# One tanh for the four LSTM gates, the output bias in two later halves, filler matmuls, and 128-row mask and bias operands in a decoder layer

## The reference

```
x = x + LSTM_attention(layernorm(x))      # LSTM of width 20 over the 56 tokens; heads give mu and sigma;
                                          # causal Gaussian weights, normalised, times layernorm(x)
x = x + cross_attention(layernorm(x), ctx_1024)   # 16 heads of 64 over 1500 context rows, plus bias bO
x = x + ffn(layernorm(x))                 # a router picks 1 of 4 experts: gelu(x W1[e] + b1[e]) Wo + bo, then layernorm
```

```
i, f, g, o = split(xg_t + h @ W_hh.T)
c = sigmoid(f) * c + sigmoid(i) * tanh(g)
h = sigmoid(o) * tanh(c)
```

## Time and profile before

| | us |
|---|---|
| median of 3 runs | 1596.07 (1593.94 to 1597.94) |
| the profiled execution's own time | 1587.43 |
| span of the profile | 1585.7 |
| PE busy | 1517.7 (96%) |
| DVE busy | 1131.3 (71%) |
| ACT busy | 903.5 (57%) |
| POOL busy | 792.8 (50%) |
| granted TensorE clock, mean | 0.985 |

### The profile page before, as it was taken

How to read it: one execution, slowest core, us unless ns; L and a number is a source line. 1 busy time by engine, 2 the same in 40 slices (tenths; PEclk the granted TensorE clock), 3 DMA queues, 4 the chain that set the end, 5 groups by cost and what they waited for, 6 DMA issues and landing times.

```text
span 1585.7 us, 25257 instructions
## 1 busy us (share of the span) xinstructions
PE 1517.7 (96%) x7555; PEld 1084.1 (68%) x7555; DVE 1131.3 (71%) x1872; ACT 903.5 (57%) x1283; POOL 792.8 (50%) x406
## 2 busy tenths in 40 slices
PE   6886899999999999999999999999999999999997
PEld 3345667777777777777777777777777777776674
DVE  4338786868686868686877778686868686868555
ACT  4335675666666666666666666666666566555311
POOL 2003365555555555656565655555555555545511
PEclk9997999999999999999999999999999999999899
DMA  4100011000000000000000000000000000100000
GB/s 157 32 0 20 1 39 40 40 39 39 32 38 28 39 28 38 30 39 39 39 39 39 39 39 39 39 39 39 39 39 39 39 39 39 40 14 7 1 1 24
DMA packets 15059, 54.92 MB, mean 35 GB/s; under 512 B 919, under 2 KB 6122, under 8 KB 15022
## 3 DMA queue, kind: packets, MB, share of 16 engines
q1 hardware_dynamic: 15022, 54.46, 9.0%
HBM read 53.54 MB, written 0.92 MB: 34 GB/s over the span
## 4 chain that ended last, share of the span: by engine, by line
PE 83%; DVE 8%; ACT 5%; issue 3%; DMA 0%; DVEq 0%; POOL 0%; POOLq 0%; ACTq 0%
PE ps L725 34%; PE ps L691 27%; PE ps L597 4%; PE ps L592 3%; PE ps L583 3%; PE ps L784 3%; DVE arena L1282 3%; PE ps L576 2%; ACT arena L982 2%; PE ps L705 2%; PE ps L512 1%; PE ps L713 1%; ACT arena L881 1%; ACT arena L884 1%; DVE arena L1268 1%
## 5 line engine op out<-in xcount | busy, mean ns | idle before, releaser
L1268 DVE TENSOR_TENSOR arena<-arena,ps 125x896 f32<-125x896 f32 x336 | 364.4, 1084 | 96.3 <-PE ps L691 96.0
L449 POOL TENSOR_TENSOR arena<-arena,ring 125x896 f32<-125x896 f32 x192 | 417.6, 2175 | 17.5 <-POOL arena L449 0.5
L691 PE MATMUL ps<-q_hi,ctxT_hi 128*125 128x448 f32 x768 | 400.0, 521 | 4.7 <-ACT arena L976 3.2
L449 POOL TENSOR_TENSOR arena<-arena 125x896 f32<-125x896 f32 x112 | 236.9, 2115 | 307.9 <-ACT arena L982 299.2
L725 PE MATMUL ps<-ring,ctx_nat 125*128 125x448 f32 x768 | 343.0, 543 | 0.0
L976 ACT ACTIVATE ring<-ps 125x896 f32<-125x896 f32 x192 | 176.5, 919 | 237.3 <-PE ps L725 149.1
L691 PE MATMUL ps<-q_hi,ctxT_lo 128*125 128x448 f32 x768 | 281.4, 366 | 0.0
L691 PE MATMUL ps<-q_lo,ctxT_hi 128*125 128x448 f32 x768 | 281.4, 366 | 0.0
L725 PE MATMUL ps<-arena,ctx_nat 125*128 125x448 f32 x576 | 242.9, 544 | 2.4
L1282 DVE TENSOR_TENSOR ring<-ring,ps 125x896 f32<-125x896 f32 x192 | 202.4, 1084 | 0.0
L691 PEld LDWEIGHTS ps<-q_hi,ctxT_hi 128*125 128x125 f32 x768 | 143.9, 187 | 66.6 <-issue 47.3
(11 more groups left out here) (201 smaller groups left out, 1879.7 us busy)
## 6 DMA issues: line engine op xcount, KB each, us to landing
ctx_raw<-in_ctx_dram SPq DMA_DIRECT2D x32, 750.0 KB
ctx_nat<-in_ctx_dram SPq DMA_DIRECT2D x32, 750.0 KB
w_sb<-in_L_ffn_W_dram SPq DMA_DIRECT2D x1, 1024.0 KB
resid<-in_x_dram SPq DMA_DIRECT2D x1, 896.0 KB, 6.0
out_dram<-ctx_raw SPq DMA_DIRECT2D x4, 224.0 KB, 2.5
ctx_raw<-in_L_xattn_WQ_dram SPq DMA_DIRECT2D x1, 512.0 KB
w_sb<-in_L_xattn_WK_dram SPq DMA_DIRECT2D x1, 512.0 KB
w_sb<-in_L_xattn_WV_dram SPq DMA_DIRECT2D x1, 512.0 KB
```

The source lines that it names most:

```text
L449: g.tensor_tensor(summed, chunk[0] if j == 1 else summed, chunk[j], ALU.add).then_inc(s["prob_added"], 1)
L691: m = mm(score_ps[j % 2][:, half, :], cx[k][:, rows], q[k][:, cols], start=(n == 0), stop=(n == 2))
L1268: v.tensor_tensor(run_max, kept(k, 0) if j == 1 else run_max, score_ps[j % 2], ALU.max).then_inc(s["maxed"], 1)
```

## The change

Six edits, the diff cut to their core:

1. LSTM: with sigmoid(z) = (1 + tanh(z/2))/2, the weights of the three sigmoid gates are halved when ACT copies them out of PSUM (seven copies for three), `h` and the cell are kept doubled, and one tanh over 20x128 serves all gates. The cell lies behind the gates in `gate_act`, so one scalar_tensor_tensor (stt) forms both products, a second one the new cell, a third `h`. The waits change their order.
2. The biases come in as columns of the raw weights, and PE turns them with the weights.
3. bO is added in two halves by POOL, behind the sums of batches 0 and 1; the wait for it moves from the first period to the first projection of each pair.
4. The three powers go behind the last sum of their period.
5. Filler matmuls of 256 columns: 2 ahead of the picking matmuls, 5 behind them, 5 ahead of the token transposes for the queries.
6. `pick_e`, `onehotT` and `b1_r` get 128 rows; ACT clears them in period 1 (`zero_pads`, six instructions).

```diff
-        gate_act = cut(4 * B, PE).rearrange("p (g b) -> p g b", g=4)
+        gate_act = cut(5 * B, PE).rearrange("p (g b) -> p g b", g=5)
+        cell = gate_act[:, 4, :]
+        cell_parts = cut(2 * B, PE).rearrange("p (g b) -> p g b", g=2)
...
-            need(sp, "biased_cleared", 2)
-            sp.dma_start(headT[PE:PE + 1, 0:NB], b_mu.rearrange("(a n) -> a n", a=1)).then_inc(s["bias_in"], 16)
...
+            for column, bias in ((PE, b_ih), (PE + 1, b_hh)):
+                sp.dma_start(w_hh_in[0:4 * PE, column:column + 1], bias.rearrange("(n a) -> n a", a=1)).then_inc(s["lstm_w_in"], 16)
...
-            need(pool, "ln_done", 2 * GROUPS)
-            g.tensor_tensor(resid_k, resid_k, bO_b[:, None, :].to_broadcast((TOK, PAIRS, D)), ALU.add).then_inc(s["bO_added"], 1)
...
-                    if isinstance(i, int) and i == PAIRS - 2 and k == 0 and j in POWERS_AT:
-                        power(3, POWERS_AT.index(j))
+                if isinstance(i, int) and i == 0:
+                    tiles = slice(k * PAIRS // 2, (k + 1) * PAIRS // 2)
+                    if k == 0:
+                        need(pool, "ln_done", 2 * GROUPS)
+                    g.tensor_tensor(resid_k[:, tiles, :], resid_k[:, tiles, :], bO_b[:, None, :].to_broadcast((TOK, PAIRS // 2, D)), ALU.add).then_inc(s["bO_added"], 1)
+                if isinstance(i, int) and i == PAIRS - 2 and k == 0:
+                    for q in range(GROUPS - 1):
+                        power(3, q)
...
-            pe.wait_ge(s["lstm_w_in"], 64)
+            pe.wait_ge(s["lstm_w_in"], 128)
...
+            def keep_busy(count, bank):
+                for n in range(count):
+                    mm(ps[:, bank, 0:WARM], ident[:], qk_w[:, 0:WARM // D, :].rearrange("p h d -> p (h d)"), start=True, stop=True)
+            need(pe, "folded_sb", H)
+            need(pe, "ctxT_lo_done", 2 * MP - 1)
+            keep_busy(2, SIDE)
...
+            keep_busy(5, SIDE)                 # behind the picking matmuls
...
+            keep_busy(5, SIDE)                 # ahead of turn_tokens(TOKEN_BANKS[1], 2, 0) and query(0, ...)
...
-            a(cell_t, cell, ACT.Sigmoid).then_inc(s["table_loaded"], 1)
+            a(cell_t, cell, ACT.Tanh).then_inc(s["table_loaded"], 1)
...
-                    a(gate_act[:, 0:3, :], gates[:, 0:3, :], ACT.Sigmoid).then_inc(s["sig_ready"], 1)
-                    a(gate_act[:, 3, :], gates[:, 3, :], ACT.Tanh).then_inc(s["tanhg_ready"], 1)
-                    need(act, "cell_step", 3 * t + 3)
-                    a(cell_t, cell, ACT.Tanh).then_inc(s["tanhc_ready"], 1)
+                    a(gate_act[:, 0:4, :], gates, ACT.Tanh).then_inc(s["tanhg_ready"], 1)
+                    need(act, "cell_step", 2 * t + 2)
+                    a(cell_t, cell, ACT.Tanh, scale=0.5).then_inc(s["tanhc_ready"], 1)
...
+            def zero_pads():
+                for n in range(2):
+                    a(b1_r[:, n, :].rearrange("p (m c) -> p m c", m=MB), ident[:, None, :].to_broadcast((128, MB, 128)), ACT.Copy, scale=0.0).then_inc(s["pads_zeroed"], 1)
+                for q in range(GROUPS):
+                    a(onehotT[q].rearrange("p (m c) -> p m c", m=G4), ident[:, None, 0:TOK].to_broadcast((128, G4, TOK)), ACT.Copy, scale=0.0).then_inc(s["pads_zeroed"], 1)
+                act.wait_ge(s["pads_zeroed"], 2 + GROUPS)
...
+                    if isinstance(i, int) and i == 0 and k == 1 and j == 9:
+                        zero_pads()
...
-                    need(dve, "sig_ready", t + 1)
-                    need(dve, "cell_step", 3 * t)
-                    v.tensor_tensor(cell_f, gate_act[:, 1, :], cell, ALU.mult).then_inc(s["cell_step"], 1)
+                    need(dve, "cell_step", 2 * t)
                     need(dve, "tanhg_ready", t + 1)
-                    v.tensor_tensor(cell_i, gate_act[:, 0, :], gate_act[:, 3, :], ALU.mult).then_inc(s["cell_step"], 1)
-                    need(dve, "cell_step", 3 * t + 2)
-                    v.tensor_tensor(cell, cell_f, cell_i, ALU.add).then_inc(s["cell_step"], 1)
+                    v.scalar_tensor_tensor(cell_parts, gate_act[:, 0:2, :], 1.0, gate_act[:, 3:5, :], ALU.add, ALU.mult).then_inc(s["cell_step"], 1)
+                    need(dve, "cell_step", 2 * t + 1)
+                    v.scalar_tensor_tensor(cell, cell_parts[:, 1, :], 0.5, cell_parts[:, 0, :], ALU.mult, ALU.add).then_inc(s["cell_step"], 1)
                     need(dve, "tanhc_ready", t + 1)
-                    v.tensor_tensor(lstm_h[0:PE, u, :], gate_act[:, 2, :], cell_t, ALU.mult).then_inc(s["h_ready"], 1)
+                    v.scalar_tensor_tensor(lstm_h[0:PE, u, :], gate_act[:, 2, :], 1.0, cell_t, ALU.add, ALU.mult).then_inc(s["h_ready"], 1)
...
+                    need(dve, "bO_added", 2)       # in add_heads, ahead of a pair's first product
...
-            need(dve, "bO_added", 1)               # ahead of the first period
```

More of the change, by code:

```diff
@@ L80, in decoder_layer @@
         bo_sb = sb("bo_sb", [D, 1])
-        pick_e = sb("pick_e", [E, E, 128], F32R)
+        pick_e = sb("pick_e", [128, E, 128], F32R)
         wr_sb = sb("wr_sb", [D, E])
@@ L134, in decoder_layer @@
         w_in = cut(D)
-        w_hh_in = cut(PE)
-        w_head_in = cut(PE)
+        w_hh_in = cut(PE + 2)
+        w_head_in = cut(PE + 1)
         wihT = cut(4 * PE)
@@ L139, in decoder_layer @@
         headT = cut(NB + 1)
-        gate_act = cut(4 * B, PE).rearrange("p (g b) -> p g b", g=4)
-        cell = cut(B, PE)
-        cell_f = cut(B, PE)
-        cell_i = cut(B, PE)
+        gate_act = cut(5 * B, PE).rearrange("p (g b) -> p g b", g=5)
+        cell = gate_act[:, 4, :]
+        cell_parts = cut(2 * B, PE).rearrange("p (g b) -> p g b", g=2)
         cell_t = cut(B, PE)
@@ L190, in decoder_layer @@
         w1_lo = [ctxT_lo[e // 2][:, e % 2 * FF:(e % 2 + 1) * FF] for e in range(E)]
-        b1_r = sb("b1_r", [E, 2, FF], F32R)
-        onehotT = [sb(f"onehotT{q}", [E, GT], F32R)[:] for q in range(GROUPS)]
+        b1_r = sb("b1_r", [128, 2, FF], F32R)
+        onehotT = [sb(f"onehotT{q}", [128, GT], F32R)[:] for q in range(GROUPS)]
         xT_halves = x_halves[:].rearrange("p (n t) -> p n t", n=2)
@@ L492, in _ @@
             pe.wait_ge(s["xT_sb"], 4)
-            pe.wait_ge(s["lstm_w_sb"], 3)
-            pe.wait_ge(s["bias_in"], 64)
+            pe.wait_ge(s["lstm_w_sb"], 7)
             pe.wait_ge(s["zeros_made"], 3)
@@ L866, in _ @@
             need(act, "zeros_made", 3)
-            a(cell_t, cell, ACT.Sigmoid).then_inc(s["table_loaded"], 1)
+            a(cell_t, cell, ACT.Tanh).then_inc(s["table_loaded"], 1)
             act.wait_ge(s["lstm_w_ps"], 1)
             need(act, "biased_cleared", 2)
-            a(wihT, ps[:, 3, 0:4 * PE], ACT.Copy).then_inc(s["lstm_w_sb"], 1)
-            a(whhT[0:PE, :], ps[0:PE, 3, 128:128 + 4 * PE], ACT.Copy).then_inc(s["lstm_w_sb"], 1)
-            a(headT[0:PE, :], ps[0:PE, 3, 256:256 + NB + 1], ACT.Copy).then_inc(s["lstm_w_sb"], 1)
+            for start, stop, half in ((0, 2 * PE, 0.5), (2 * PE, 3 * PE, 1.0), (3 * PE, 4 * PE, 0.5)):
+                a(wihT[:, start:stop], ps[:, 3, start:stop], ACT.Copy, scale=half).then_inc(s["lstm_w_sb"], 1)
+                a(whhT[0:PE + 2, start:stop], ps[0:PE + 2, 3, 128 + start:128 + stop], ACT.Copy, scale=half / 2).then_inc(s["lstm_w_sb"], 1)
+            a(headT[0:PE + 1, :], ps[0:PE + 1, 3, 256:256 + NB + 1], ACT.Copy, scale=0.5).then_inc(s["lstm_w_sb"], 1)
             for q in range(GROUPS):
@@ L1017, in copy_onehot @@
                 need(act, "onehotT_ps", q + 1)
-                a(onehotT[q], ps[0:E, bank, 0:GT], ACT.Copy).then_inc(s["onehotT_sb"], 1)
+                a(onehotT[q][0:E], ps[0:E, bank, 0:GT], ACT.Copy).then_inc(s["onehotT_sb"], 1)
+            def zero_pads():
[4 more added lines that the diff above has]
+                act.wait_ge(s["pads_zeroed"], 2 + GROUPS)
             def side_copies(i, k, j, places):
@@ L1060, in period @@
                         act.wait_ge(s["ffn_w_in"], 16 * 7)
-                        a(b1_r[:, 0, :], b1_sb[:], ACT.Copy).then_inc(s["b1_hi_done"], 1)
+                        a(b1_r[0:E, 0, :], b1_sb[:], ACT.Copy).then_inc(s["b1_hi_done"], 1)
                 assert not slot_work(i, k, CH - 1) or last
```

28 lines of the change are left out of this document (13 added, 15 removed).

## The result

The changed kernel takes 1572.82 us in the median (1571.64 to 1573.78, 4 runs) against 1596.11 (1593.94 to 1597.94) of the kernel before in the same job: ratio 0.9859, 95% interval 0.9837 to 0.988. The forecast was 1586.1, range 1579 to 1593. The profiled execution took 1573.70 us (span 1571.9), so between the two profiled executions the spans differ by 13.8 us only. Both gaps need explaining: 10.0 against 13.8 inside the traces, and 13.8 against 23.3 between traces and medians.

A forecast was written before the change was run, and what follows sets the result against it. PE was taken as the limit (83% of the chain of waits), except in three stretches. The terms summed to -10.0 against the profiled 1587.43, giving 1577.4; with 8.64 carried over, 1586.1 us, range 1579 to 1593.

The forecast's parts named there:

- LSTM: LSTM steps: one activation, earlier handover and stt save 0.14 us a loop step, 5.6 over forty; -6.1 us in all.
- table load: ACT behind the LSTM: sigmoid at line 925 needs a table load of its own, +0.7 us, otherwise 0.
- fillers: Around picking and queries: filler matmuls fit PE's idle time, taken as 0, bounds -0.8 to +1.0 us.
- output bias: Second q_lo: without POOL's bias addition beside it, the first maximum starts 2.4 us sooner, bounds 0 and -3.2.
- pads' clearing: Period 1: clearing takes 3.9 us of ACT and delays PE by 0 to 3.9, taken as +1.0 us.
- FFN's start: From b1's first matmuls to the second sums: wider operands keep the clock up, -3.2 us, bounds 0 and -6.8.
- The offset: Whole kernel: the runs' median was 8.64 us above the profiled execution; this difference was carried over unchanged.
- Powers: Behind their period's sums: the powers leave POOL's sums and still come before DVE's scaling, so 0.
- the first: Rival at the pads: the clock falls as before, wider operands only cost clearing; -6.8 us, 1589.3, chance 0.15.
- The second: Rival, whole kernel: LSTM, table, picking, bias, period 1 and tail all go well; -15.3 us, 1580.8, chance 0.18.
- The third: Rival: the LSTM's stt hands over late and ACT blocks period 1; -3.6 us, 1592.5, chance 0.09.
- The fourth: Rival in LSTM steps: a small stt costs more than a product; +26 us against forecast, 1612, chance 0.05.

The follow-up runs named there:

- variant with narrow operands: The best kernel with the mask and b1 matmuls both back on 4 rows, clearing left at the start: 1583.7 us, ratio 0.9934.
- the kernel before again: The kernel before, unchanged, profiled and timed a second time: 1593.8 us, ratio 0.9995.
- the output bias alone: The kernel before with only the output bias in halves and the moved powers: 1589.57 us, ratio 0.9969.
- the pads' own run: The kernel before with only the 128-row mask and b1 operands and their clearing in period 1: 1580.23 us, ratio 0.9916.
- the early clearing: The changed kernel with its six clearing copies moved from period 1 to ACT's waits at the start: 1569.79 us, ratio 0.9857.
- the best kernel: The early clearing plus first table load by sigmoid, fillers in the last six LSTM steps and between token transposes: 1566.83 us; again 1565.79.
- the LSTM's own run: The kernel before with only the LSTM edit and the biases as columns: 1590.46 us, ratio 0.9978.
- the narrow masks' run: The best kernel with only the mask matmuls back on 4 rows, b1 still on 128: 1572.71 us, ratio 0.9881.

## Why the prediction was wrong, step by step

Offsets between the two first profiles, at marks that both have:

| term of the sum | forecast | measured |
|---|---|---|
| LSTM, to the heads (125.10, 121.34) | -6.1 | -3.8 |
| table load, to DVE's first difference (129.46, 126.07) | +0.7 | +0.4 |
| fillers, to the first score (155.75, 152.36) | 0 | 0.0 |
| output bias, to the first maximum (160.82, 156.65) | -2.4 | -0.8 |
| pads' clearing, to period 2's first weighing (305.53, 307.51) | +1.0 | +6.2 |
| periods 2 to 30 (1427.47, 1425.70) | 0 | -3.8 |
| FFN's start, to the second sums (1503.10, 1498.10) | -3.2 | -3.2 |
| behind it, to the end (1585.7, 1571.9) | 0 | -8.8 |
| sum, profiled to profiled | -10.0 | -13.8 |
| profiled execution to median | +8.64 | -0.88 |

- **The offset: the step that failed first.** "The runs' median is 8.64 higher, and the trace doesn't say where; I carry the difference over." That carried a difference between executions over as if it were a constant of the kernel. It accounts for 9.5 of the 13.3 us between forecast and result. The profiled execution was a short one, and a large part of what lengthens the others is what the change removes. The variant with narrow operands shows it by its times: 9 us in the median above its own shortest run, at a lower clock. The profiles show where. From the second sums to the end, the six with 4-row masks and b1 take 82.6 us, or 88.6 in two of them (the kernel before again, and the output bias alone), where the clock falls three times; the pads' own run, the changed kernel, the early clearing and the best kernel take 73.8 to 74.2, and no fall begins there ahead of the last 9 us, which are at half clock in part in every profile. So some 6 of the 8.64 can be such falls. The rest is not placed: the first eight LSTM steps alone take 17.0 to 20.2 us from profile to profile, with operands of either kind, and the pads' own run spread over 14 us.
- **The tail: counted as 0.** The forecast gave the wide operands one effect, the clock, at one place. At the other b1 groups and at the masks the clock of that trace was full, so nothing was counted. The rows at full clock had the price in their starts (0.60 a pair, 0.80 the three behind it); I had not read them. -8.8: in all these profiles the stretch takes 82.6 us without a fall and 73.8 to 74.2 with wide operands, and putting the 4 rows back costs 9.0.
- **The FFN's start: the number right, the step behind it wrong.** "If the wider operands keep the clock" took the fall at 1489.4 for the work of the 4-row operands. The next profile of the same kernel has the clock full up to the first sums, and so have the other four with 4-row masks and b1. POOL's last addition frees the first sums 30.9 us behind the last turning of the maxima in every kernel with the sums in that place, but for the first profile of before (31.6); what wider operands save PE ahead of it becomes waiting (3.08, forecast 1.5). From that turning to the second sums the five take 37.0 to 38.6 us and the profiles with wide operands 36.7 to 38.4; the first of before takes 40.0. The -3.2 is that one profile's long fall, so luck. The 2 us for a fall had no row behind it; the fall that came, 3.4 us at half clock, costs 1.7.
- **Clearing: the direct cost right, its consequence missed.** 3.0 us of ACT (forecast 3.9), 0.95 of PE (forecast +1.0). Then the sums stand close together at half clock for ten us: another 5. Shown by the early clearing.
- **LSTM: loop steps right** (-5.2 for -5.6), the unrolled ones wrong. The last seven take 13.33 us for 12.19: DVE now comes 0.10 behind ACT for 0.02, and the clock falls from 111.9. With fillers there, clock full, they take 12.56 in the best kernel, so 0.77 goes with the clock, and 0.37 is left, for which the handover, 0.08 a step, is the likely cause. That the order of the waits causes the handover is not tried. The start cost 0.25.
- **Table load:** comes, as taken; smaller, as it starts ahead of the heads. A sigmoid first removes it (0.37).
- **Output bias:** right at full clock (-2.3 alone); here the clock fell at 152.9 under the first scores, and 1.5 came back.
- **Fillers: right**, 0; they move a fall, they do not remove it.
- **Powers:** forecast 0, measured -0.9. The other 3.0 between periods 2 and 30 is a fall at 1376.6: period 29 takes 46.0 us in the first profile of before, 43.0 in the second. -0.9 is shown, and the -3.0 is not shown to be the change's. It is luck as far as the second profile tells; but the single runs of LSTM, bias and pads have 45.8, 44.3 and 44.6 there, and no profile of the changed kernel or its variants has more than 43.0, so the cause stays open.

Of the rivals the first falls by its price: the wider operands do not only cost their clearing, they gain some 8.7 us where neither kernel has a fall. That they also hold the clock is supported behind the second sums, where a fall begins in four of the eight profiles with 4-row masks or b1 and in none of the eight with 128 rows in both (the last 9 us left out); at the FFN's start, where the forecast put it, it is not shown. The second, all going well, had the sign of the error but 8 us too little, since it kept the same offset and the same empty tail. The third came half: the step of 1.70 speaks against its late handover, but period 1 cost 6.2, more than its 3.9. The fourth falls with the step. Rule and rows on the clock: PE is busy 3.40 of 3.40 us in the windows above at half clock. The Trainium skill (TensorE: Matmul & The Clock Gate, What's actually happening) has the clock follow how busy PE was; busy by the profile's count these stretches are, so that rule does not say which fall. The rows tell what runs at the falls, transposes, one-column sums or 4-row matmuls among full ones, but the same work also runs at full clock (1520:1540 above), so they do not say which fall either.

## What to carry to other kernels

Before a forecast is put on the median, look at several executions: if the profiled one is the shortest and the mean granted clock differs between runs, the offset is a cost of its own that a change can remove, and it must not be carried over. Nor should a cause be read out of a fall that only one profile has: the one at 1489.4 was gone in the next profile of the same kernel. Read PE's cost from start to start across a change of shape, not from the mean of a line: the 0.2 us at each change of rows sat half in the neighbours' line. And where an edit delays PE by one us among thin matmuls, price the fall that may follow (here five us), and put such an edit where its engine already waits.

## What the runs showed of the hardware that was not expected

- Matmuls over 4 or 64 rows between matmuls over 128 cost the same 0.4 us a pair more, two changes of some 0.2, and a single one over 4 rows 0.3 (32 rows: the whole kernel's time is that of 4). 128 rows with zeros in them cost nothing of the kind.
- PE fully busy does not mean full clock: 10.00 of 10.00 us busy at 0.50 in period 1, 6.80 of 6.80 at 0.51 in the kernel before.
- Beside POOL's long addition of bO, DVE's q_lo, which reads two tensors in SBUF, is stretched: 4.32 us beside 5.41 us of POOL, two of them in 5.58 beside 4.51 in the LSTM's own run, 1.09 each without. No run tries which operand matters.
- From the first gates to the ninth step the LSTM takes 17.0 to 17.2 us in nine profiles, 18.5 to 18.6 in six, and 19.7 and 20.2 in the runs with narrow masks and with the pads alone. The granted clock reads 1.00 there in all, yet in 20:25 PE works off 34 matmul records in the narrow masks' run and 50 in the best kernel's. No edit goes with it; the cause is open.
- The kernel with b1 on 32 rows took 5143.93 us in its profiled run and 1571.63 to 1575.32 in the four timed ones. In it every kind of matmul is long (line 706: 1527 ns in the mean, against 520 in the best kernel's) at a granted clock that reads 1.00 throughout; its page has no row for the clock, so that reading may stand for none. No other run showed this; its cause is open.
